# Router logits by a product with stationary weights, and three turns of the result

## What is computed

```python
logits = x @ gate_w.T                     # [3072, 512] x [512, 64]
scores = jax.nn.softmax(logits, axis=-1)
topk_w, topk_i = jax.lax.top_k(scores, K) # K = 6
...
pos = jnp.zeros((TK,), jnp.int32).at[order].set(pos_sorted.astype(jnp.int32))
valid = pos < CAP
slot = jnp.where(valid, pos, CAP)
```

## Time and profile before

| | us |
|---|---|
| median of 3 runs | 1705.49 |
| lowest and highest | 1704.61, 1706.07 |
| the profiled execution | 1706.95 |
| its span, first to last instruction | 1705.3 |
| mean granted TensorE clock in it | 0.840 |

### The profile page before, as it was taken

How to read it: one execution, slowest core, us unless ns; L and a number is a source line. 1 busy time by engine, 2 the same in 40 slices (tenths; PEclk the granted TensorE clock), 3 DMA queues, 4 the chain that set the end, 5 groups by cost and what they waited for, 6 DMA issues and landing times. The chain is left out here.

```text
span 1705.3 us, 23870 instructions
## 1 busy us (share of the span) xinstructions
PE 1368.9 (80%) x9120; PEld 843.2 (49%) x9120; DVE 759.1 (45%) x1633; ACT 404.9 (24%) x676; POOL 424.6 (25%) x455
## 2 busy tenths in 40 slices
PE   3094788879788788887978840499999999999994
PEld 2094452434426254352533430366666666666673
DVE  7982545455555656456455331332232222232231
ACT  2021123333333233333333410211111111111110
POOL 3000110100242223324233446122222222222221
PEclk8597675877969688696877965699999999999997
DMA  3022221323213242221323140888989989898882
GB/s 97 0 66 72 52 50 35 73 54 91 75 34 80 54 111 55 68 63 37 94 54 94 53 163 21 261 308 248 320 277 282 297 261 327 249 328 267 266 251 31
DMA packets 129837, 239.54 MB, mean 140 GB/s; under 512 B 58056, under 2 KB 64088, under 8 KB 129752
## 3 DMA queue, kind: packets, MB, share of 16 engines
q1 hardware_dynamic: 114232, 214.16, 40.4%
q0 software_dynamic: 15520, 24.22, 7.0%
HBM read 175.66 MB, written 38.90 MB: 126 GB/s over the span
## 5 line engine op out<-in xcount | busy, mean ns | idle before, releaser
L951 DVE TENSOR_REDUCE at_maxes<-at_ps 128x1 f32<-128x384 f32 x384 | 196.4, 553 | 131.3 <-PE at_ps L664 122.6
L808 ACT ACTIVATE bulk<-at_ps 128x1152 f32<-128x1152 f32 x128 | 144.9, 1132 | 367.4 <-PE at_ps L634 367.1
L1313 PE MATMUL mo_ps<-mo_x2s,mo_sgu 128*117 128x384 f32 (+1 forms) x1152 | 221.2, 344 | 0.0
L1313 PEld LDWEIGHTS mo_ps<-mo_x2s,mo_sgu 128*117 128x117 f32 (+1 forms) x1152 | 198.7, 181 | 13.4 <-issue 13.1
L1534 POOL DMA_INDIRECT out_rows<-mo_y,mo_scatter_ix x64 | 91.4, 1428 | 399.6 <-DMA out_rows<-mo_y,mo_scatter_ix 226.1
L664 PE MATMUL at_ps<-at_qb 32*128 32x384 bf16 x384 | 125.7, 442 | 78.6 <-DVE at_maxes L951 59.5
L1114 POOL DMA_INDIRECT slot_table<-at_toki,at_si x144 | 141.2, 981 | 51.0 <-issue 48.3
L664 PEld LDWEIGHTS at_ps<-at_qb 32*128 32x128 bf16 x384 | 28.6, 96 | 211.0 <-DVE at_maxes L951 173.5
L624 PE MATMUL at_ps<-WxT,at_xT 128*128 128x512 f32 (+1 forms) x576 | 114.0, 351 | 17.4 <-ACT at_v L853 15.6
L634 PE MATMUL at_ps<-at_QT 97*128 97x384 f32 x384 | 115.5, 416 | 6.9 <-ACT bulk L808 6.9
L1076 POOL TENSOR_TENSOR at_oTs<-at_oT,at_oTs 128x384 fp32r<-128x384 f32 x32 | 32.1, 1002 | 352.0 <-ACT at_oTs L820 352.0
(11 more groups left out here) (198 smaller groups left out, 1700.0 us busy)
## 6 DMA issues: line engine op xcount, KB each, us to landing
mo_wgu<-in_L_ffn_w_gate SPq DMA_DIRECT2D x32, 704.0 KB
mo_wgu<-in_L_ffn_w_up SPq DMA_DIRECT2D x32, 704.0 KB
bulk<-in_L_ffn_w_gate SPq DMA_DIRECT2D x32, 704.0 KB, 7.3
bulk<-in_L_ffn_w_up SPq DMA_DIRECT2D x32, 704.0 KB, 8.6
mo_wd<-in_L_ffn_w_down SPq DMA_DIRECT2D x32, 512.0 KB
bulk<-in_L_ffn_w_down SPq DMA_DIRECT2D x32, 512.0 KB, 5.4
at_QT<-at_qhi SPq DMA_DIRECT2D x64, 192.0 KB
rows_scores<-at_x SPq DMA_DIRECT2D x8, 864.0 KB, 3.7
```

The source lines that it names most:

```text
L808: A.activation(PT[:, N % RING, :, :], ps[:, 0:NT, 0:SEQ], ACT.Exp, scale=float(HD) ** -0.5)\
L951: V.tensor_reduce(maxes[:, s, h:h + 1], ps[:, 5 + u % 2, 0:SEQ], AX.X, ALU.max, negate=True)\
L1313: m = M.matmul(ps[0:SW[c], 5 + g, 0:SEQ], sgu[:, wa, g, k, SO[c]:SO[c] + SW[c]], x2s[:, xa, k, :], start=(k3 == 0), stop=(k3 == 3 * KC - 1))
```

## The change

The product of the router is turned around. The weights `gwT`, 128x64 for each quarter of the width, are stationary, and all 384 turned rows of `x2T` move in one product, so 4 products take the place of 12, and their result is 64 x 384: experts in the partitions. ScalarE copies it to a new tile `lgT`, three turns (`turn_logits`) bring it back to tokens in the partitions in the old place in bank 7, and ScalarE copies that to `lg` as before. To make room, each later step of the router moves by one slot, other than the product itself and the last step in slot 9.

```diff
             def logits(d):
                 pe.wait_ge(x2T_ready, KC * (d + 1))
+                for k in range(KC):
+                    m = T.matmul(ps[0:E, 7, 0:SEQ], gwT[:, k, :], x2T[:, k, :], start=(k == 0), stop=(k == KC - 1))
+                m.then_inc(logitsT_ready, 1)
+
+            def turn_logits(d):
+                pe.wait_ge(lgT_copied, d + 1)
                 for s in range(NT):
-                    for k in range(KC):
-                        m = T.matmul(ps[:, 7, s * E:(s + 1) * E], x2T[:, k, s * P:(s + 1) * P], gwT[:, k, :],
-                                     start=(k == 0), stop=(k == KC - 1))
+                    m = T.transpose(ps[:, 7, s * E:(s + 1) * E], lgT[:, s * P:(s + 1) * P], ident[0:E, 0:E])
                 m.then_inc(logits_ready, 1)
...
                     if prev2 and n == 0:
                         logits(d)
+                    if prev2 and n == 1:
+                        turn_logits(d)
...
-                    if prev2 and n == 4:
+                    if prev2 and n == 5:
                         places(d)
...
                     if prev2 and n == 1:
+                        act.wait_ge(logitsT_ready, d + 1)
+                        A.activation(lgT[:], ps[0:E, 7, 0:SEQ], ACT.Copy).then_inc(lgT_copied, 1)
+                    if prev2 and n == 2:
                         act.wait_ge(logits_ready, d + 1)
...
-                    if prev2 and n == 3:
+                    if prev2 and n == 4:
                         act.wait_ge(gmax_ready, d + 1)
```

In `routing(d, n)` of VectorE the slots 1, 2, 4 and 5 become 2, 3, 5 and 6, and `places(d)` of GpSimd moves from slot 6 to slot 7:

```diff
-                if n == 2:
+                if n == 3:
                     for s in range(NT):
                         ins = V.tensor_tensor(
...
-                if n == 5:
+                if n == 6:
                     dve.wait_ge(pos_ready, d + 1)
...
-                    if prev2 and n == 6:
+                    if prev2 and n == 7:
                         places(d)
```

More of the change, by code:

```diff
@@ L474, in attention_phase @@
         x2T = sb("at_x2T", [P, KC, SEQ])
+        lgT = sb("at_lgT", [E, SEQ])
         lg = sb("at_lg", [P, NT, E])
@@ L511, in attention_phase @@
         x2_turned, x2T_ready, logits_ready, lg_copied = sem("x2_turned"), sem("x2T_ready"), sem("logits_ready"), sem("lg_copied")
+        logitsT_ready, lgT_copied = sem("logitsT_ready"), sem("lgT_copied")
         gmax_ready, gexp_ready, mask_ready = sem("gmax_ready"), sem("gexp_ready"), sem("mask_ready")
@@ L983, in routing @@
             def routing(d, n):
-                if n == 1:
+                if n == 2:
                     dve.wait_ge(lg_copied, d + 1)
@@ L1002, in routing @@
                     V.tensor_copy(mask[:], pos[:]).then_inc(mask_ready, 1)
-                if n == 4:
+                if n == 5:
                     dve.wait_ge(gexp_ready, NT * (d + 1))
```

## The result

| | before | after |
|---|---|---|
| median of 22 runs each, us | 1705.57 | 1709.05 |
| lowest and highest | 1699.59, 1709.17 | 1703.79, 1717.18 |
| the profiled execution | 1706.95 | 1710.43 |
| its span | 1705.3 | 1708.8 |

The account below looks back on a forecast made before the run. TensorE's work and waits bound the attention phase (80% busy). Five full iterations +0.5, iteration 7 -1.3, iteration 8 +1.5 make +0.7, so 1706.2 us; forecast band 1702 to 1709 (0.46), range 1700.5 to 1715.5.

Parts of the forecast that it names:

- rival A: Full iterations: the new wait at project_out(0) stays whole, the clock gives nothing back; +7.0, 1712.5 us; chance with D 0.37.
- (a): Router product in slot 0: 4 products of 384 columns replace 12 of 64, -0.15 us (bounds 0 and -0.3).
- Rival C: Router product much cheaper, half of what L1355 shows: -1.3 us in each of 5 iterations, 1699.7 us; chance 0.04.
- (b): Slot 1: TensorE waits some 0.3 us for ScalarE's logits copy, then turns three tiles; +0.43 us together with (a).
- (c): Slot 3: v's copy no longer stands behind the router's exponentials, and rope of k comes earlier; -1.00 us.
- Rival D: Slot 3: v's copy still waits because rope_k is late; +1.0 us an iteration; chance 0.37 together with A.
- (d): Slots 4 and 5: TensorE's nine products of places move behind the last kv projection; nothing in the sum.
- (e): Slot 6: project_out(0) waits for pos_read behind rope and statistics, about 1.9 us; sum there +1.35 us.
- (f): Slot 7: the clock no longer falls at project_out(1), -1.54 us (bounds 0 and -1.54).
- Iteration 7: No projections ahead: one-hot work moves behind the divide, so the values start earlier; -1.3 us, down to -2.5.
- Iteration 8: No scores, one chain from logits copy to project_out(0): copy, value products and turn lengthen it; sum +1.5 us.
- B: Full iterations: the clock gains more than the wait costs, or positions are read earlier; -6.8, 1698.7 us; chance 0.13.

Follow-up runs that it names:

- e10: The changed kernel with the turned router product done twice in a row in slot 0; one execution, 1730.37 us.
- e7: e3 with the three turns of the logits moved behind project_q in slot 1; 1704.43 us, ratio 0.9994 to the kernel before.
- e3: The changed kernel with VectorE reading the positions ahead of the next sequence's statistics in slot 6; 1703.94 us, ratio 0.9997 to the kernel before.
- e6: The changed kernel with the positions read later, in slot 7 behind the divide; 1727.22 us, ratio 1.0129 to the kernel before.
- e8: The kernel before with 18 unread bf16 products added in slot 7 where TensorE would wait for q_lo; 1704.18 us, ratio 0.9993.
- e1: The changed kernel with the old product, without turn and second copy, later slots kept; 1711.22 us, ratio 1.0028 to the kernel before.
- e2: The kernel before with the turned product, copy and turn, every other router step in its old slot; 1714.30 us, ratio 1.0044.
- e4: e1 with the positions read ahead of the next sequence's statistics; 1700.98 us, ratio 0.9979 to the kernel before.
- e5: The kernel before with one-hot work, exponentials and scores a slot later only where there is attention, positions later only in iteration 7; 1692.96 us, ratio 0.9929.
- e11: e2 with e5's slots, second copy and maxima in slot 2 where there is attention; 1700.45 us, ratio 0.9977 to the kernel before.
- e9: The kernel before with the old router product done twice in a row in slot 0; one execution, 1734.18 us.

## Why the prediction came out as it did

The time lies in the range, and its sign is on the edge: 1709.05 against the forecast's 1706.2, between it and rival A. The waits of a full iteration were right, the clock was not, and that the total came so near is in part luck. The steps one by one:

- **(a), predicted -0.15, measured +0.04.** The price of 0.64 us a product, from L1355, was right to 0.01 (e10: 2.58 for four). Mis-sized is the hand-over, on both sides. The scores' loads start 2.72 after the first load of the new product, for in e10 they come 0.74 after its last load, over twice the pitch of 0.32; and before they started after 2.68 (618.76 in the trace), not after the 2.75 that the loads' row gives. That takes the gain away. Rival C fell with this: a float32 product of 384 columns is two records of 0.32. The Trainium skill, "FP8 and Floating Point Precision", section "TensorE Precision Notes", counts four passes for true float32; at 2.4 GHz four times 384 columns are 0.64 us by estimate, and the trace agrees. By the gap rule weighed in the prediction the eight records would take 1.30 us; they take 2.58, twice that. (The rate of the loads that the prediction gives with that rule stands on its page in the section behind the one named, and entered no sum.)
- **(b), predicted +0.43 with (a), measured +0.65.** 0.19 of the gap is (a). The wait and the copy's 0.47 us were right, and the turn takes 0.33 in place of 0.28. e7 adds that hiding the wait gains only 0.1.
- **(c), predicted -1.00, measured -0.98.** v's copy no longer waits for the exponentials, and the rope was there in time. Rival D fell.
- **(d), nothing in the sum.** As predicted.
- **(e), predicted 1.92 with +1.35 at project_out(0), measured 1.68 with +1.43.** Later work by (a) and (b) came off the wait. The mechanism is shown by e3, which cuts it to 0.54, and e6, which doubles it. One slip: iteration 6 has no statistics of a next sequence, so there the delay is 0.26 only. Rival A's five times 1.35 should have been four.
- **(f), predicted that the clock stays up in slot 7 of every full iteration, -1.54 each.** This is the step that failed. It stayed up in two of five, and in one of these the clock then took 2.8 us back by staying low to the next product. The halves behind the turned heads give -1.3 in sum where the forecast needed some -6. The pull towards equal periods exists (e3 and e7 start the heads 0.2 us later than before, e8 saves 1.5, and all have 102.4), but it swallows gains as well as small delays, and of a delay of 1.5 and 1.4 it gave back only 0.3 and 0.5 in iterations 2 and 5 (in 6, where the delay is 0.26, all of it). So the five iterations came to +4.7 in the trace, where I had +0.5 with +2 as the bound.
- **Iteration 7, predicted -1.3 (to -2.5), measured -2.85.** The divide ahead of the one-hot work did what was said, and the values' wait fell by 1.76 (2.74 to 0.98). Most of the rest is the clock, which the prediction had only as a bound (-2.5): before has it at 0.50 from 932.6 to 936.0, and after has no fall there. From the product to the values after is 1.10 shorter, from there to project_out(0) 1.23, of which 0.73 are the value products; the last 0.5 lies behind that, and its cause isn't shown. The periods of iteration 7 split by this fall: 53.6 to 55.9 in the four kernels that have it in that stretch (before, e1, e2, e8), 51.7 to 52.7 in the six that don't (after, e3, e4, e5, e7, e11).
- **Iteration 8, predicted +1.5, measured +2.73.** Mis-sized: I counted the longer way to the logits but not that the divide (982.23 to 984.20) now stands ahead of the one-hot work there, on the only chain. e5, which keeps the old slots in this iteration, has a period of 41.10, as before. Four kernels besides before show it up to project_out(0), which starts 13.25 after the product before, 14.54 in e2 and 14.62 in e11 (turned, old order here), 15.82 in e1 (old product, new order) and 15.98 in after. So product and turn alone cost 1.3 to 1.4, near the forecast; the order alone costs 2.6; and together they cost 2.7, since the two delays overlap. The periods (41.07, 41.77, 41.74, 42.51 and 43.80) differ less in e1, e2 and e11, because there project_out(0) takes 4.3 to 4.9 us for the 5.46 that it takes in before and after, where the lower clock lasts through it. What part of the order's price is the divide and what the later slots isn't shown apart.
- **Iteration 9, predicted 0.** GpSimd's scatters covered it, to 0.01 us.
- **B** fell: no iteration of after gains 1.2 on the forecast of -0.2.

The two errors of iterations 7 and 8 (-1.5 and +1.2) nearly cancel, which is luck. What was left was (f): +4.7 in place of +0.5, outside its own bounds. In the trace the start that came 1.03 earlier took some of that away. So the result is near A without A's full price: +6.0 of first halves less 1.3. The two halves of the change don't add: the slots alone cost 6 us in the medians (5 by the ratio, e1), the product alone 9 (7.5 by the ratio, e2), both together 3.5 (4 by the ratio). In the first halves they do add (+0.78 and +0.65 give +1.43); it is the clock's part that doesn't.

## What to carry to other kernels

Price a matmul with turned operands by what sets its pace on either side, the weight loads or the moving columns times the passes of its type, not by its number of instructions: 12 float32 products of 64 columns behind 128-column loads and 4 of 384 columns cost the same 2.7 us here, and the way back (a copy and three turns) is then all loss. When a step is moved to make room, look at what now stands ahead of it on its engine before it raises a semaphore, and in each kind of iteration by itself: the same move was worth -1 us where other work hid it and up to +2.6 us where nothing did. Where the clock falls in every iteration, a saving just ahead of a fall is not money in hand; run several executions and compare whole periods before counting it.

## What the runs showed of the hardware that was not expected

- After a float32 product with 64 stationary columns the next group's first load is late: 0.60 us idle on the load side and 0.74 from the last load, where the loads inside the product are 0.32 apart. Behind the old product the scores' loads follow without an idle time of their own in e9.
- A saving of 1.5 us at one place (e8) can vanish whole: the lower clock came one projection later, the saving was gone when that projection ended, and the period stayed 102.4.
- The granted clock can stay low for 51 us while TensorE is busy 43.8 of them (e2), and whether it does differs between iterations of one execution and, as the mean granted clocks of e2's runs suggest (0.823 to 0.860), between executions: e2's runs spread over 15 us, those of e5 over 4. Two such rises missing cost 2.8 us; the first of them missing alone cost nothing.
- Three turns of 64x128 float32 take 0.33 us in a row when their operand has just been copied, and together with the turned product they cost 0.55 when they stand between a projection and the scores (e7).
